# A binary convolution and gated state-space block over sixteen images: one reload buffer given to x, channel sums next to the gating, and sign bands shifted by one row, one unit ahead

## Chip, cores and metric

The kernel runs on one core of one Trainium2 chip. The metric is the device time of one execution in microseconds (us).

## What is computed

x is 16 x 112 x 112 x 256 in fp32. There are two layers, both with a residual:

```python
# _gn: normalize over H, W and 8 channels (32 groups)
x = x + _L0_conv_ref(_gn(x), L0_conv_kernel)   # depthwise 3x3 of sign(x) with sign(kernel)
x = x + _L1_conv_ref(_gn(x), ...)
# _L1_conv_ref(x): m, max over channels after a channel gate (sigmoid of two small
# matmuls on spatial mean and max); a scan over the 12544 pixels of an image with 16
# states gives y; a 7x7 convolution of channel mean and max gives s;
# x2 = xc * sigmoid(y) + xc * sigmoid(s); batch norm over all images; gamma, beta; relu
```

Only the sign of the group-normalized x enters the first convolution, that is, x compared with its group's mean.

## The kernel before, in words

Channels lie on the 128 partitions, in two halves (`j` = 0, 1). Pixels lie along the free dimension. The program has three blocks: the first reads x, makes x1 = x + convolution, writes it to `x1_scratch` in DRAM and computes the channel features; the second runs the scan of the second group of images and the batch statistics; the third computes and writes the output. The change is in the first block.

An image is cut into two parts, upper and lower half (`part`), and each part into seven units of eight rows (`u`, `RT` = 8, `TP` = 896 pixels). A convolution handles both parts at once: a sign element holds sign(upper) + 1024 * sign(lower) in fp16, so one matmul serves both parts. `image(i)` exists for each engine as a loop over `h` = 0 to 13 with `u, j = divmod(h, 2)`. What the engines do at pass h of image i, in the order of the code:

- PE: the convolution of (u, j), 18 matmuls (L1338), into `turn[h % 2]`; in the middle of it (from h = 2 on) the transposes of tile 2(h-2) of image i+1 (`turn_tile`, L1244); then the channel sums of strip h-5 (`channel_sums`, L1277); the transposes for the maximum over channels of the same strip (`blocks_back`, L1291); then tile 2(h-2)+1 of the next image. After h = 13 the last four tiles, `blocks_back` and `channel_sums` of strip 9, and the group means (L1250).
- ACT: evacuates the tile (L750), packs the convolution (L758), copies the channel sums (`average`, L813), evacuates the second tile, squares x1 of the unit before (L766), gates strip h-3 (`apply_gate`, L795 and L799).
- DVE: signs (`make_signs`, L961 and L976) of unit u+2, the maximum of the two channel halves of strip h-4 (`max_halves`, L1117), reductions over channels of strip h-5 (`reduce_blocks`, L1128), adds the convolution to x and takes the maximum (L1022, L1028), and gates one channel half of strip h-3 (`gate_half`, L1107) when the strip's number is 2 to 9. For the other strips ACT gates both halves. At h = 9 come three reductions of sign counts over edges (L985 to L990), then small steps that end in the sum of the convolution.
- SP: issues all DMAs, in order: the x load for a later pass (`load_next_x`, L569), the store of unit h-1 (L589), the load of strip h-1 (`load_g`, L584), and the channel sums of two strips to DRAM (L594).

A "strip" is 896 pixels of the image before (all 256 channels), read back from `x1_scratch` for gating, since the gate needs the statistics of the whole image. `strip_at(i, h, lag)` gives the strip h - lag of image i-1, and for h < lag one of image i-2. Strips live in a ring of four buffers `xg` in `xc`; x lives in a ring of three buffers in `stage`, which starts again with each image. A load into the strip ring waits until maximum and sum of the strip four back are made; an x load waits until the tiles of three loads back are turned. The channel sums of strip c go to `turn[c % 2]`, so at pass h to the half that the convolution of this pass doesn't use, once that has been packed.

After h = 13 DVE runs `image_sums`, `reduce_blocks` of strip 9, `sums_of_x` (L942) and `mean_of_x` (L951) of the next image, then signs of (0, 0) and (1, 0), `image_squares`, signs (0, 1), `image_variance`, signs (1, 1) and `attention_inputs`, which makes `fc_in`. Between variance and attention inputs ACT computes a logarithm and an exponential. PE's `hidden` matmul (L1260) in h = 1 waits for `fc_in`; the tile of h = 2 waits for `gate_argument` (DVE, L1083), which runs in h = 1 behind the signs of that pass.

In the first image, all 14 x loads and 28 tiles come ahead of the loop, and SP then issues the small parameter loads (`scol`, L612: 40 of them) and the bands before it enters `image(0)`. In the last image there is no next x; PE and DVE do parts of the second stage for the first group of images instead (a spatial convolution, `delta_step`).

## Time and profile before

| | us |
|---|---|
| median of 3 runs | 3481.12 |
| lowest and highest | 3471.48, 3544.35 |
| the profiled execution's own time | 3476.38 |
| its span, first to last instruction | 3474.7 |
| mean granted TensorE clock (share of full) | 0.832 |

The profile is of one execution. PE is the matmul engine, DVE the vector engine, ACT the scalar engine, POOL GpSimd and SP the engine that issues DMAs. In a timeline each line has the start in us from the span's beginning, the duration (overlaps with the next are possible), engine, line of the kernel, operation, output and inputs with their shape, and in brackets the idle time before it and what ended it.

### The profile page before, as it was taken

Reading aid. Unit: us, or ns where it says so; the run is one execution under the profiler, and the core shown is the slowest. Engines: PE = TensorE matmul, PEld = TensorE weight load, DVE = VectorE, ACT = ScalarE, POOL = GpSimd, SP = SyncE. Lnnn points to the kernel's source line nnn. Section 1 sums busy time; section 2 is a strip of 40 time slices with the busy share of each in tenths; the row PEclk is TensorE's granted clock in tenths of the full one; section 3 lists DMA queues with packets and bytes.
Section 4 is the critical chain, followed back from the end, with each engine's and each line's share of the span. In section 5 each row is a group of like instructions: output and inputs, shape, how many; then the busy total and the mean of one; then the engine's idle time right before and its main releaser. Section 6 shows DMA issues by size and latency. Waiting matters only on the chain. (4 is left out here: it accounts for less than half of the span.)

```text
span 3474.7 us, 50996 instructions
## 1 busy us (share of the span) xinstructions
PE 2596.4 (75%) x17105; PEld 1661.0 (48%) x17105; DVE 3053.3 (88%) x4395; ACT 2693.6 (78%) x3748; POOL 19.9 (1%) x23
## 2 busy tenths in 40 slices
PE   4899999999999998999877333333377767777676
PEld 3565555655556555566443010000255555555555
DVE  5689989999999998999886599999898899899997
ACT  3788887878888888888674287777788888888887
POOL 1000000000000000000000000000000000000000
PEclk8999999999999999999998555555577787777777
DMA  5898888988889888898765399999499999999998
GB/s 177 316 406 346 352 340 355 396 343 351 350 353 404 350 347 344 350 405 346 254 205 133 87 414 416 416 416 414 198 423 427 427 418 418 419 419 421 420 421 340
DMA packets 258888, 1227.99 MB, mean 353 GB/s; under 512 B 36421, under 2 KB 45537, under 8 KB 244353
## 3 DMA queue, kind: packets, MB, share of 16 engines
q1 hardware_dynamic: 258688, 1225.40, 89.0%
q8 instruction: 117, 1.92, 0.2%
q14 instruction: 83, 0.67, 0.1%
HBM read 805.14 MB, written 420.17 MB: 353 GB/s over the span
## 5 line engine op out<-in xcount | busy, mean ns | idle before, releaser
L1338 PE MATMUL psum<-signs,taps 128*128 128x448 f16 x4032 | 876.6, 362 | 49.1 <-DVE signs L976 44.9
L1759 PE MATMUL psum<-ident,xt 128*128 128x128 f32 x3136 | 560.5, 348 | 281.0 <-ACT stage L1793 232.5
L1759 PEld LDWEIGHTS psum<-ident,xt 128*128 128x128 f32 x3136 | 498.7, 212 | 367.2 <-ACT stage L1793 309.2
L1439 PE MATMUL psum<-signs,picked 12*128 12x448 bf16 x896 | 328.8, 510 | 356.1 <-DMA signs<-gate_scratch 287.3
L1338 PEld LDWEIGHTS psum<-signs,taps 128*128 128x128 f16 x4032 | 395.3, 100 | 381.0 <-issue 48.1
L1793 ACT ACTIVATE stage<-psum 128x512 f32<-128x512 f32 x784 | 407.1, 612 | 173.7 <-DMA out_dram<-stage 149.4
L1814 DVE SCALAR_TENSOR_TENSOR xc<-xt,curs,psum 128x1792 f32<-128x1792 f32 x224 | 456.1, 2077 | 85.7 <-PE psum L1439 81.2
L750 ACT ACTIVATE xt<-psum 128x896 f32<-128x896 f32 x416 | 377.9, 912 | 162.9 <-PE psum L1244 162.7
L1623 DVE SCALAR_TENSOR_TENSOR xc<-xt,curs,psum 128x1792 f32<-128x1792 f32 x224 | 455.6, 2078 | 49.5 <-PE psum L1439 34.4
L1244 PE MATMUL psum<-ident,stage 128*128 128x128 f32 x3136 | 416.5, 277 | 76.6 <-DMA stage<-x_dram 43.7
L1561 ACT ACTIVATE xc<-xc 128x1792 f32<-128x1792 f32 x224 | 380.1, 1697 | 113.6 <-DVE xc L1623 113.6
L1829 DVE TENSOR_TENSOR xt<-xc,xt 128x1792 f32<-128x1792 f32 x224 | 442.6, 2018 | 0.0
L1028 DVE CUSTOM_DVE_ANT_0 xt<-scratch,xt 128x896 f32<-128x896 int8 (+1 forms) x416 | 436.1, 1085 | 0.0
L1244 PEld LDWEIGHTS psum<-ident,stage 128*128 128x128 f32 x3136 | 364.9, 143 | 118.7 <-DMA stage<-x_dram 50.2
L1781 ACT ACTIVATE xc<-xc,bn,curs 128x1792 f32<-128x1792 f32 x224 | 411.3, 1900 | 8.6 <-DVE xc L1814 8.4
L766 ACT ACTIVATE hsum<-xt,nmean 128x1792 bf16<-128x1792 f32 x208 | 370.4, 1781 | 0.7
L1439 PEld LDWEIGHTS psum<-signs,picked 12*128 12x128 bf16 x896 | 86.7, 117 | 562.5 <-DVE xc L1623 380.1
L1128 DVE TENSOR_REDUCE pmax<-psum 128x4 f32<-128x512 f32 x448 | 257.7, 617 | 73.3 <-PE psum L1291 73.2
L758 ACT ACTIVATE scratch<-psum,border 128x896 int16<-128x896 f32 x224 | 223.9, 1000 | 82.8 <-PE psum L1338 82.4
L1117 DVE TENSOR_TENSOR stage<-xc 128x896 f32<-128x896 f32 x224 | 243.9, 1089 | 27.4 <-ACT xc L795 19.5
L976 DVE SCALAR_TENSOR_TENSOR signs<-xt,mean,signs 128x896 f16<-128x896 f32 x208 | 240.3, 1155 | 7.4
L1291 PE MATMUL psum<-ident,stage 128*128 128x128 f32 x1568 | 223.8, 282 | 24.1 <-ACT pmax_rows L806 13.8
(199 smaller groups left out, 2205.9 us busy)
## 6 DMA issues: line engine op xcount, KB each, us to landing
xt<-x_scratch SPq DMA_DIRECT2D x210, 1792.0 KB
stage<-x_dram SPq DMA_DIRECT2D x224, 896.0 KB, 9.0
out_dram<-stage SPq DMA_DIRECT2D x112, 1792.0 KB, 13.7
xc<-x_scratch SPq DMA_DIRECT2D x210, 896.0 KB, 8.3
x_scratch<-xt SPq DMA_DIRECT2D x208, 896.0 KB, 7.5
x_scratch<-last_unit SPq DMA_DIRECT2D x16, 896.0 KB, 6.9
signs<-ssm_scratch SPq DMA_DIRECT2D x28, 448.0 KB, 4.6
signs<-gate_scratch SPq DMA_DIRECT2D x217, 10.5 KB
```

The costliest lines, as they stand in the source:

```text
L750: nc.scalar.activation(dst, src, ACT.Identity, scale=PACK if part else 1.0, accum_out=xsum_p[:, j, 2 * u + part:2 * u + part + 1]).then_in ...
L1028: nc.vector.tensor_tensor_reduce(out=px, in0=conv, in1=px, scale=1.0 / PACK if part else 1.0, scalar=-3.0e38, op0=ALU.add, op1=ALU.max, ac ...
L1244: ins = nc.tensor.transpose(ring[:, t * P:(t + 1) * P], xin[b][:, t, j * P:(j + 1) * P], ident[:, :])
L1338: return nc.tensor.matmul(turn[h % 2][:, b * 512:b * 512 + HB], taps[:, j, t, :], signs[:, j, r:r + RT // 2, dw:dw + W], start=t == 0, sto ...
L1439: last = nc.tensor.matmul(dst[:, b, :], picked[:, b * P:(b + 1) * P], gate_rows[:, s * BW:(s + 1) * BW], start=True, stop=True)
L1561: nc.scalar.activation(u, u, ACT.Square, accum_out=g2_p[:, n, j, bass.ds(it, 1)]).then_inc(squared3, 1)
L1623: nc.vector.scalar_tensor_tensor(fours(xc[n % 2][:, j, :]), fours(slots[s][:, j, :]), curs[:, h, j:j + 1], gate_ps3[n % 2], ALU.add, ALU.mult,
L1759: last = nc.tensor.transpose(out_ps[k % 4][:, v * C + j * P:v * C + (j + 1) * P], block_in, ident[:, :])
L1781: nc.scalar.activation(u, u, ACT.Relu, bias=bn[:, 7, j:j + 1], scale=curs[:, h, NJ + j:NJ + j + 1]).then_inc(relu_made, 1)
L1793: nc.scalar.activation(outs[n % 2][:, 2 * k:2 * k + 2, :].rearrange("p t c -> p (t c)"), out_ps[k % 4], ACT.Identity).then_inc(staged, 1)
L1814: nc.vector.scalar_tensor_tensor(fours(xc[n % 2][:, j, :]), fours(slots[s][:, j, :]), curs[:, h, j:j + 1], gate_ps4, ALU.add, ALU.mult).th ...
L1829: nc.vector.tensor_tensor(x1, u, x1, ALU.add).then_inc(x2_made, 1)
```

## The change

It has three parts. (1) `xin` gets a fourth buffer, the second half of `xc[1]`, and the strip ring shrinks from four buffers to three. The x ring now runs on across images, each x load is issued one pass earlier relative to its use, and the first x load of the next image goes out in pass 13; for image 1 it goes out ahead of the small parameter loads. (2) `channel_sums` and `average` of a strip come one pass earlier (lag 4 for 5); `sum_ps` takes the other half of `turn` by strip number, which at a given pass is the same as before. The sum of strip 9 thereby moves from the image's end into pass 13. (3) A sign band is shifted down by one row, so that band u ends with the row below unit u: band 0 has nine rows, bands 1 to 4 have eight, band 5 has seven and band 6 seven; the first row of unit 6 gets two instructions of its own with a count of their own (`NS + 8`), since it may lie in another buffer. Band u is all that the convolution of unit u needs beside the earlier ones, so bands are made one unit ahead: passes 1 to 11 make one each, three are made at the image's start in place of four. The edge reductions go from pass 9 to 11, the count steps from passes 10 to 13 to passes 12 and 13.

```diff
+        NX = 4
...
         xg = [xc[b // 2][...][:, b % 2 * SP:(b % 2 + 1) * SP].rearrange(
-            "p (j n) -> p j n", j=NJ) for b in range(4)]
+            "p (j n) -> p j n", j=NJ) for b in range(3)]
+        xin.append(xc[1][:, :, :].rearrange("p j n -> p (j n)")[:, SP:2 * SP].rearrange("p (t c) -> p t c", c=C))
...
         def sum_ps(c):
-            return turn[c % 2][:, 0:SQ]
+            return turn[(c + 1) % 2][:, 0:SQ]
...
         def sign_at(u, j):
-            return 2 * j + u if u < 2 else NJ * u + j
+            return NJ * u + j
...
                 def load_next_x(i, k):
-                    sp.wait_ge(turned, i * NTILE + 2 * (k - 3) + 2)
+                    sp.wait_ge(turned, i * NTILE + 2 * (k - NX) + 2)
                     load_x(i, k)
...
-                    if i * NP + c >= 4:
-                        sp.wait_ge(maxed, i * NP + c - 3)
-                        sp.wait_ge(summed, i * NP + c - 3)
+                    if i * NP + c >= 3:
+                        sp.wait_ge(maxed, i * NP + c - 2)
+                        sp.wait_ge(summed, i * NP + c - 2)
...
-                for p in range(3, NP):
+                for p in range(NX, NP):
                     load_next_x(0, p)
+                load_next_x(1, 0)
 
                 for src, col in ((A_d[0, :], 0), (B_w_d[:, 0], 1), (B_b_d, 2), (C_w_d[:, 0], 3), (C_b_d, 4)):
...
                     if more:
-                        sp.wait_ge(turned, i * NTILE + NTILE)
-                        for p in range(3):
-                            load_x(i + 1, p)
+                        for p in range(1, NX):
+                            load_next_x(i + 1, p)
                     for h in range(NP):
-                        if h >= 3 and more:
-                            load_next_x(i + 1, h)
+                        if h >= NX - 1 and more and (i + 2 < NB or h < NP - 1):
+                            load_next_x(i + 1 + (h + 1) // NP, (h + 1) % NP)
...
             # ACT
-                        if (at := strip_at(i, h, 5)) and h >= 1:
+                        if at := strip_at(i, h, 4):
                             average(*at)
...
                     square(i, NU - 1, 1, first)
-                    if more and channels:
-                        average(i - 1, 9)
                     inverse_deviation(i)
...
             # DVE
-                    for u in range(NS):
+                    for u in (*range(NS), NS + 8):
                         nc.vector.tensor_reduce(coef[:, :, part, u], kval[:, :, :], AX, ALU.add).then_inc(coef_steps, 1)
...
+                def band_rows(u):
+                    return u * RT + (u > 0), (u + 1) * RT + (u < NU - 2)
...
+                    if u == NU - 2:
+                        row = signs[:, j, 1 + (NU - 1) * RT:2 + (NU - 1) * RT, 1:1 + W]
+                        compare(row, x_rows(i, j, NU - 1, 1, 0, 1), mean64[:, j:j + 1], ALU.mult, PACK).then_inc(row_steps, 1)
+                    r0, r1 = band_rows(u)
+                    rows = signs[:, j, 1 + r0:1 + r1, 1:1 + W]
+                    compare(rows, x_band(i, j, u, 1), mean64[:, j:j + 1], ALU.mult, PACK).then_inc(sign_steps, 1)
+                    if u == NU - 2:
+                        dve.wait_ge(row_steps, i * NJ + j + 1)
+                        nc.vector.scalar_tensor_tensor(
+                            row, x_rows(i, j, NU - 1, 0, 0, 1), mean, row, ALU.is_ge, ALU.add,
+                            accum_out=counts[:, j, NS + 8:NS + 9])
                     dve.wait_ge(sign_steps, base + 1)
                     nc.vector.scalar_tensor_tensor(
-                        rows, x_rows(i, j, u, 0, 0, RT),
+                        rows, x_band(i, j, u, 0),
                         mean, rows, ALU.is_ge, ALU.add, accum_out=counts[:, j, u:u + 1]).then_inc(signs_made, 1)
...
-                        if u + 2 < NU:
-                            make_signs(i, u + 2, j)
+                        if h >= 1 and u + 1 < NU:
+                            make_signs(i, u + 1, j)
...
-                        if h == 9:
+                        if h == 11:
                             edge_counts(i)
...
                         make_signs(i + 1, 0, 0)
-                        make_signs(i + 1, 1, 0)
+                        make_signs(i + 1, 0, 1)
                     image_squares(i)
                     if more:
-                        make_signs(i + 1, 0, 1)
+                        make_signs(i + 1, 1, 0)
                     image_variance(i)
-                    if more:
-                        make_signs(i + 1, 1, 1)
                     attention_inputs(i)
...
             # PE
-                        pe.wait_ge(signs_made, i * NP + sign_at(u if u == 0 else min(u + 1, NU - 1), j) + 1)
+                        pe.wait_ge(signs_made, i * NP + sign_at(u, j) + 1)
                         if not (first and h < 2):
                             pe.wait_ge(unpack_in, i * NP + h - 1)
-                        if strip_at(i, h, 6):
-                            pe.wait_ge(averaged, (i - 1) * NP + h - 5)
+                        if strip_at(i, h, 5):
+                            pe.wait_ge(averaged, (i - 1) * NP + h - 4)
...
-                            pe.wait_ge(signs_made, i * NP + sign_at(1, j) + 1)
                             for t in range(9):
...
-                        if (at := strip_at(i, h, 5)) and h >= 1:
+                        if at := strip_at(i, h, 4):
                             pe.wait_ge(unpack_in, i * NP + h)
                             channel_sums(*at)
+                        if (at := strip_at(i, h, 5)) and h >= 1:
                             blocks_back(*at)
...
                         if channels:
                             blocks_back(i - 1, 9)
-                            pe.wait_ge(evacuated, (i + 2) * NTILE)
-                            channel_sums(i - 1, 9)
                         group_sums(i + 1)
```

## Rows read from the trace of the kernel before

**Rows 1.** The page: busy us (share of the span) x instructions.
```profile
PE 2596.4 (75%) x17105; PEld 1661.0 (48%) x17105; DVE 3053.3 (88%) x4395; ACT 2693.6 (78%) x3748; POOL 19.9 (1%) x23
```

**Rows 2.** Busy time of each engine in one stretch, granted clock, DMA share, GB/s.
```profile
950.00:1060.00 110.00, 101.65 (x813) 64.95 (x811) 101.42 (x208) 91.98 (x143) 0.00 (x0) 0.98 0.92 362
```

**Rows 3.** Timeline of DVE: start, us, line, idle before. An image's first sum.
```profile
258.40 0.17 DVE L942 TENSOR_REDUCE xsum<-xsum_p 128x4 f32<-128x28 f32 x1
...
1014.54 0.18 DVE L942 TENSOR_REDUCE xsum<-xsum_p 128x4 f32<-128x28 f32 x1
...
1662.09 0.17 DVE L942 TENSOR_REDUCE xsum<-xsum_p 128x4 f32<-128x28 f32 x1
```

**Rows 4.** Timeline of DVE, units 5 to 9 of that image.
```profile
1065.21 0.74 DVE L1107 TENSOR_SCALAR xc<-xc,cur,gbias 128x896 f32<-128x896 f32 x1
1072.06 0.74 DVE L1107 TENSOR_SCALAR xc<-xc,cur,gbias 128x896 f32<-128x896 f32 x1
...
1092.60 0.62 DVE L985 TENSOR_REDUCE counts<-signs 128x4 f32<-128x448 f16 x1
1093.68 0.75 DVE L1107 TENSOR_SCALAR xc<-xc,cur,gbias 128x896 f32<-128x896 f32 x1
```

**Rows 5.** Timeline of PE, units 5, 6 and 12.
```profile
1060.38 0.55 PE L1291 MATMUL psum<-ident,stage 128*128 128x128 f32 x3 [1.06 <-ACT pmax_rows L806]
1065.82 0.96 PE L1277 MATMUL psum<-xc,over_c 128*32 128x224 f32 x16
...
1106.47 0.96 PE L1277 MATMUL psum<-xc,over_c 128*32 128x224 f32 x16
```

**Rows 6.** Timeline of PE and ACT, unit 4.
```profile
1050.78 0.96 PE L1277 MATMUL psum<-xc,over_c 128*32 128x224 f32 x16
...
1053.54 0.92 ACT L750 ACTIVATE xt<-psum 128x896 f32<-128x896 f32 x1 [0.32 <-PE psum L1244]
...
1057.25 1.12 ACT L799 ACTIVATE xc<-xc,gbias,cur 128x896 f32<-128x896 f32 x1
1058.28 0.90 ACT L750 ACTIVATE xt<-psum 128x896 f32<-128x896 f32 x1
```

**Rows 7.** Timeline of PE, ACT and DVE, from one image into the next.
```profile
1011.18 1.75 PE L1244 MATMUL psum<-ident,stage 128*128 128x128 f32 x14 [0.98 <-DMA stage<-x_dram]
1014.08 1.13 ACT L795 ACTIVATE xc<-xc,gbias,cur 128x896 f32<-128x896 f32 x1
1015.88 1.07 DVE L961 TENSOR_SCALAR signs<-xt,mean 128x112 f16<-128x112 f32 x3
1027.04 0.25 PE L1260 MATMUL psum<-fc_in,w 128*16 128x2 f32 x4 [0.95 <-DVEq L1076]
1027.08 0.69 DVE L961 TENSOR_SCALAR signs<-xt,mean 128x896 f16<-128x896 f32 x1
1028.89 1.08 DVE L1117 TENSOR_TENSOR stage<-xc 128x896 f32<-128x896 f32 x1
1034.28 0.98 PE L1244 MATMUL psum<-ident,stage 128*128 128x128 f32 x7 [0.73 <-DVEq L1084]
```

**Rows 8.** Waits of PE between 110 and 1800 us: in total, times, longest.
```profile
PE psum L1244 <- DMA stage<-x_dram: 18.8, 12, 2.4
```

**Rows 9.** Timelines of SP's queue and of PE, images 0 and 1.
```profile
48.92 7.03 SPq L612 DMA_DIRECT2D scol<-A_dram  x8
78.84 3.02 SPq L569 DMA_DIRECT2D stage<-x_dram  x3
87.23 1.75 PE L1244 MATMUL psum<-ident,stage 128*128 128x128 f32 x7 [11.72 <-DMA stage<-x_dram]
93.11 2.09 PE L1338 MATMUL psum<-signs,taps 128*128 128x448 f16 x10
98.08 2.07 PE L1338 MATMUL psum<-signs,taps 128*128 128x448 f16 x10
```

**Rows 10.** The page, DMA issues: count, KB each, median us to landing.
```profile
xc<-x_scratch SPq DMA_DIRECT2D x210, 896.0 KB, 8.3
```

More of the change, by code:

```diff
@@ L235, in binary_conv_then_gated_ssm_block @@
         taps_made = sem("taps_made")
-        x_in = [sem(f"x_in{b}") for b in range(3)]
+        x_in = [sem(f"x_in{b}") for b in range(NX)]
         turned = sem("turned")
@@ L266, in binary_conv_then_gated_ssm_block @@
         gate_in = sem("gate_in")
-        g_in = [sem(f"g_in{b}") for b in range(4)]
+        g_in = [sem(f"g_in{b}") for b in range(3)]
         gated = sem("gated")
@@ L603, in _ @@
                     sp.dma_start(dst[:], src).then_inc(params_in, 16)
-                for p in range(3):
+                for p in range(NX):
                     load_x(0, p)
                 sp.dma_start(lsa[:, :], lsa_d.broadcast_to([H, KS * KS * 2])).then_inc(lsa_in, 16)
-                for p in range(3, NP):
+                for p in range(NX, NP):
                     load_next_x(0, p)
+                load_next_x(1, 0)
                 for src, col in ((A_d[0, :], 0), (B_w_d[:, 0], 1), (B_b_d, 2), (C_w_d[:, 0], 3), (C_b_d, 4)):
@@ L862, in _ @@
                 apply_gate(NB - 2, 11)
-                average(NB - 2, 9)
                 gate_exp(NB - 1)
@@ L907, in _ @@
                 for part in range(2):
-                    for u in range(NS):
+                    for u in (*range(NS), NS + 8):
                         nc.vector.tensor_reduce(coef[:, :, part, u], kval[:, :, :], AX, ALU.add).then_inc(coef_steps, 1)
-                    steps.n += NS
+                    steps.n += NS + 1
                     row = NS + part
@@ L961, in compare, with x_band @@
                     return nc.vector.tensor_scalar(dst, x, mean, v, ALU.is_ge, op1)
+                def x_band(i, j, u, part):
+                    if u == NU - 1:
+                        return x_rows(i, j, u, part, 1, RT)
+                    r0, r1 = band_rows(u)
+                    at = part * H2 * W
+                    return xt[:, j, at + r0 * W:at + r1 * W].rearrange("p (h w) -> p h w", w=W)
+                def band_rows(u):
+                    return u * RT + (u > 0), (u + 1) * RT + (u < NU - 2)
                 def make_signs(i, u, j):
@@ L1133, in _ @@
                 mean_of_x(0)
-                for h in range(4):
-                    make_signs(0, h % 2, h // 2)
+                for h in range(NJ + 1):
+                    make_signs(0, *divmod(h, NJ))
                 def image(i):
@@ L1393, in _ @@
                 hidden(NB - 1)
-                channels_late(NB - 2, 9)
+                blocks_back(NB - 2, 9)
                 gate(NB - 1)
```

37 lines of the change are left out of this document (17 added, 20 removed).

## Prediction

> **What bounds the kernel now.** I read the page's busy times first: DVE is busy for 88% of the span, more than any other engine [rows 1]. Such shares mix stages, so next I took windows of equal length over the first part of the program. In each the granted clock is 0.97 or 0.98 and both PE and DVE are above 90%, as in the one shown: 101.65 and 101.42 of 110 us [rows 2]. The change touches only this part, which ends near 1780 us. Then I timed one image by the DVE instruction that starts an image's group means: from 258.40 to 1662.09 us are 13 images, 107.98 us each, and one of them starts at 1014.54 [rows 3]. The timelines of PE, DVE and ACT inside that image say what sets its length. I call one pass of the loop over h (one channel half of a unit) a unit here.
>
> From unit 6 on DVE repeats its work every 6.85 us with no idle time (its gate_half at 1065.21 and at 1072.06) [rows 4]. PE starts its channel sums at 1065.82 in unit 6 and at 1106.47 in unit 12, 6.78 us a unit [rows 5]. Both are full; DVE falls 0.07 us a unit behind PE, which costs nothing since it makes no signs in units 10 to 13 and catches up there. In units 2 to 5 ACT gates both channel halves and is full too; it waits 0.32 us in the unit shown [rows 6]. Between images there is a chain: transposes (0.98 us late for an x load), evacuations, means, signs, PE's convolution, and later PE's waits for fc_in and for gate_argument [rows 7].
>
> **The change part by part.** All is compared with the profiled execution: span 3474.7 us, time 3476.4 us, which is 4.7 us below the median of the runs, 3481.1.
>
> *1. x loads one unit ahead, within an image.* PE waited for x 12 times between 110 and 1800 us, 18.8 us in all and 2.4 at most [rows 8]. These lie at ends of images, where the last tiles follow each other with no convolution between, as at 1011.18 [rows 7]. The load now goes out a unit (6.8 us) sooner, more than the longest wait, so I take the waits as gone. What is late next is ACT: it evacuates the last tiles one after another until 1014.08, which ends at best 0.1 us sooner, while the means began at 1014.54 [rows 3, 7]. So of a wait of 0.98 only some 0.49 comes back, and I take off 0.49 from each: 18.8 - 12 x 0.49 = 12.9 us gained. Bounds: 0 (the load comes no sooner) and 18.8.
>
> *2. The first image's small loads.* After image 0's last x load SP issues 40 loads of one column each and a few more, from 48.92 us on, and image 1's first three x loads only at 78.84; PE stood still 11.72 us for them until 87.23 [rows 9]. Now image 1's first x load goes out ahead of the small ones. PE can do the unit that uses it, and then waits for the second one, still behind them. One unit there is 98.08 - 93.11 = 4.97 us [rows 9]: 5 us gained. The start itself has four loads in flight instead of three, and SP comes to the small loads when 22 tiles are turned, with one load less ahead of it at some 2.3 us (0.92 MB at 400 GB/s). I take 3 us, between 0 and 5. Together 8 us (5 to 10).
>
> *3. Signs one unit ahead, at the image's start.* DVE makes three bands there instead of four. The two nine-row bands take some 0.17 us more each. One band of 1.8 us (1027.08 to 1028.89 is one [rows 7]) goes from in front of fc_in, but it was also the work that covered ACT's logarithm and exponential, now open with 0.5 us. So fc_in comes 1.8 - 0.5 - 0.2 = 1.1 us sooner than 1027.04. Unit 1 ends that much sooner on PE; then a wait of 0.40 us for the maximum goes, and the one of 0.73 us at 1034.28 for gate_argument, since no band stands ahead of it. Unit 2 is about 2.1 us ahead.
>
> *4. Channel sums right after gating.* PE now waits in unit h for gating that ACT and DVE finish at the end of their unit h-1. Queued behind that wait on PE are blocks_back and the turn of tile n+1, for which ACT's next evacuation waits: a closed loop. Its length from rows 6: channel sums to evacuation 1053.54 - 1050.78 = 2.76 us, from there to the end of both gatings 1058.28 - 1053.54 = 4.74 us. That is 7.5 us with both halves, and 1.03 less, 6.5, with one. The latter stays under PE's 6.78. The former exceeds ACT's own work in such a unit (4.74 and some 2.2 for the other evacuation, pack and average: 6.9) by up to 0.6 in units 3 and 4, and PE first meets the wait 0.8 us late; in unit 5 it waited 1.06 us for the maximum's rows anyway [rows 5]. Of the 2.1 us ahead 1.5 are given back: unit 6 starts 0.6 us ahead, at 1065.2.
>
> *5. DVE becomes part of the loop.* From unit 6 to 13 channel sums also wait for DVE's gate_half of the unit before; so far DVE could be late there for free. It now has bands in units 10 and 11, the three edge reductions (1093.68 - 1092.60 = 1.08 us [rows 4]) in unit 11 instead of 9, and two extra row instructions for each channel half in units 8 and 9. A row compare adds 0.19 us (1015.88: two of them and a band's compare of 0.69 in 1.07 [rows 7]); the row's sum with its accumulator I take at 0.25. The bands of these units and the last two are a row shorter, 0.2 us less. From the end of unit 5 to that of unit 11: 2 x 6.85 + 2 x (6.85 + 0.44 - 0.2) + 2 x 6.65 + 1.08 = 42.3 us. Unit 5 ends on DVE near 1063.9: its last reduction follows the blocks that PE makes after the wait of unit 5, now 0.6 us sooner than 1060.38 and done at 1060.3, and 3.6 us of DVE's own work come after. So unit 12's sums start at 1063.9 + 42.3 + 0.1 = 1106.3, against 1106.47 before [rows 5]: all but 0.2 us is given back. With bands and reductions shared out over two channel halves and 14 full images I count 0, with bounds of -1.2 us an image (DVE not binding, the head start kept) and +1.2 us (0.1 to 0.2 us of latency a unit in the loop): -17 and +17 us.
>
> The Trainium skill speaks against my price for the rows. Its page "VectorE: DVE Perf Modes", section "The TRN2 errata — SBUF-src ops pay a fixed extra latency per instruction", has a fixed part of about 150 cycles at 0.96 GHz. For 112 elements that makes 0.27 us, an estimate, and four an image 1.1 instead of 0.9: 3 us more over the kernel. The 0.19 us at 1015.88 disagrees, for compares issued back to back.
>
> *6. A ring of three for the gated strips.* A strip's load now waits for the maximum of the strip three back, made 1.5 us later in the unit than the sum it used to wait for, and SP stands still with store and x load queued behind it. Some one and a half units remain until the gating, over a landing time of 8.3 us [rows 10]. At an image's start one such load moves by some 12 us, to about 1027; its strip is gated after 1040. I count nothing; without that cover each image would lose some 2 us.
>
> *7. The rest.* Moved count steps lie on DVE's idle time in units 12 and 13, the added reductions for coef under image 0's loads. After the last image the strip load that waited for sum 9 waits for maximum 10, 1.5 us later, against one channel sum less on PE: nothing. In the last image DVE also computes the deltas and binds more: 1.5 us lost, bounds 0 and 4. All after 1830 us is unchanged.
>
> Sum: 3476.4 - 12.9 - 8 + 0 + 1.5 = 3457.0.
>
> **Rivals.**
> *A, the loop of parts 4 and 5 costs more (slower than before).* Its place is PE's wait ahead of channel sums in the units that gate one half there. For it: DVE's gate_half of 1065.21 ends after PE's channel sums of 1065.82 have begun, and DVE's unit is longer than PE's [rows 4, 5]. Against: ACT's loop of 6.5 leaves 0.2 us. With 0.25 us more in ten units it is 2.5 us an image, 35 us over 14: 3457 + 35 = 3492. From 1.4 us an image on the change is no gain.
> *B, DVE doesn't bind.* If PE and ACT set units 6 to 13 and DVE follows, the head start survives, 1.2 us an image: 3457 - 17 = 3440. Against: DVE shows no idle time in units 6 to 9.
> *C, the extra x buffer brings no earlier x.* Three transfers of 0.92 MB in a unit of 6.78 us are 406 GB/s. If the DMA engines can't give more, the waits stay and only the 5 us of part 2 remain: 3471. Against: their share is 0.92, not 1, with a mean of 362 GB/s over a window that holds an image's end, where little is moved [rows 2]. On this the page "DMA: Bandwidth & Descriptors", section "Where 436 GB/s comes from", of the Trainium skill says that transfers between HBM and SBUF are held to about 358 GB/s. By that rule C would hold; the trace's 362 as a mean disagrees.
>
> **How the numbers follow.** Forecast 0.5, A 0.15, B 0.17, C 0.18. The forecast's own range is 3445 to 3470; B reaches down to 3440, C up to 3471, A to 3492. For 8 in 10 I take 3434 to 3488. A measurement of this kernel tells about 2% from no change, 70 us. Only B with three times its price would reach that: 0.04. Slower by 70 us needs over 6 us an image in A: 0.04. Within 2%: 0.92.
>
> **What would show it.** Right: PE's waits for x at image ends are gone and images lie near 107.1 us apart; the stop at 87 us is near 6 us long and one unit later; PE waits ahead of channel sums, for ACT in units 3 and 4 and for DVE from unit 9 on, up to 1 us in unit 12; DVE has no idle time from unit 6 to 11. Wrong: images of 109 us with those waits longer (A), images under 106.3 (B), x waits as before (C), or a lower granted clock in the first part.

## The result and the profile after

The change makes the kernel slower. The median went from 3476.3 us (4 runs, with those above) to 3609.02 us (3608.52 to 3660.04); the ratio is 1.042, with a 95% interval of 1.036 to 1.049. By the medians alone it is 1.038. The forecast was 3457 us, with a range from 3434 to 3488: both the sign and the size were wrong. Some executions of one and the same kernel take 1 to 2% longer at a lower mean granted clock, such as the one of 3660 us here (0.812 against 0.819); the medians take them in, and the ratios leave out those that are over 1.5% above the fastest. The profiled execution took 3608.6 us, with a span of 3606.9.

Where the time is can be read from three instants. These are the DVE instructions that start an image's group means, the same as in [rows 3], in the timeline of DVE of the changed kernel:

```profile
242.08 0.18 DVE L943 TENSOR_REDUCE xsum<-xsum_p 128x4 f32<-128x28 f32 x1
...
1071.95 0.18 DVE L943 TENSOR_REDUCE xsum<-xsum_p 128x4 f32<-128x28 f32 x1
...
1778.61 0.18 DVE L943 TENSOR_REDUCE xsum<-xsum_p 128x4 f32<-128x28 f32 x1
```

The first stands 16.3 us earlier than its partner of 258.40: what lies before image 2 became shorter. From the first to the last are the same 13 images, 118.19 us each, where it was 107.98: 132.8 us lost. From the last to the end of the span are 1828.3 us, where it was 1812.6: 15.7 lost in the last image and what follows it. The three make 132.2 us, the difference of the two spans.

The page's busy lines of PE and DVE and the window that answers to [rows 2] show engines that have become idle, not busier. DVE's 3053.3 us have grown by 50, but its share has fallen from 88 to 86%:

```profile
PE 2622.9 (73%) x17105; PEld 1679.9 (47%) x17105; DVE 3102.9 (86%) x4493; ACT 2695.7 (75%) x3748; POOL 19.7 (1%) x23
```

```profile
950.00:1060.00 110.00, 94.88 (x736) 60.75 (x735) 96.84 (x198) 82.82 (x130) 0.00 (x0) 0.94 0.88 327
```

PE and DVE are each some 5 to 7 us shorter of work in 110 us, and the DMA's share and the granted clock are lower. So a wait has come in. The view of waits from 110 to 1800 us (total, times, longest) names it:

```profile
PE psum L1354 <- ACT hsum L817: 96.4, 28, 8.1
ACT hsum L817 <- DMA feat_scratch<-hsum: 91.8, 13, 8.6
DVE stage L1137 <- ACT xc L803: 90.5, 14, 8.4
```

Three engines wait some 7 us each, once an image (the first row's 28 times hold short ones too): one event, passed on. The reader should look for the one that waits for no engine. That is ACT's `average` (L817), which waits for a DMA, the store of strip sums. The timeline around one of them, of SP, ACT, PE and DVE:

```profile
1112.06 1.07 SPq L598 DMA_DIRECT2D feat_scratch<-hsum  x1
...
1118.88 0.36 ACT L817 ACTIVATE hsum<-psum 128x224 f32<-128x224 f32 x1 [7.15 <-DMA feat_scratch<-hsum]
...
1119.38 3.89 PE L1354 MATMUL psum<-signs,taps 128*128 128x448 f16 x10 [6.65 <-ACT hsum L817]
...
1123.98 1.09 DVE L1137 TENSOR_TENSOR stage<-xc 128x896 f32<-128x896 f32 x1 [7.03 <-ACT xc L803]
```

SP issues the store at 1112.06, and ACT is released at 1118.88, 6.8 us later: the store's landing time. After it PE's convolution of ten matmuls takes 3.89 us, where it takes 2.08 elsewhere. The mean granted clock from 1119 to 1123 us is 0.50, which is the lower level, 1.2 GHz; from 1100 to 1112, ahead of the pause, it was 1.00.

This is the cause in the code. There are two strip-sum buffers, `srow[s % 2]`, and an image has seven pairs of strips. So its last pair (s = 6) and the next image's first (s = 0) use the same buffer. `sums_out` of pair 6 goes out in pass 4 (even passes, lag 6). `average` of strip 0, which needs the buffer back, came in pass 5 before and comes in pass 4 now. The pass between the two had been the cover of the store's landing.

The second loss stands in DVE's groups with the shapes kept apart (busy, mean ns of one, idle before). L962 is the compare of a band, and 1008, 896 and 784 elements are nine, eight and seven rows of 112:

```profile
L962 DVE TENSOR_SCALAR signs<-xt,mean 128x896 f16<-128x896 f32 x128 | 87.8, 686 | 4.5 <-DVE gbias L1117 0.6
...
L962 DVE TENSOR_SCALAR signs<-xt,mean 128x784 f16<-128x784 f32 x48 | 49.3, 1028 | 0.0
...
L962 DVE TENSOR_SCALAR signs<-xt,mean 128x1008 f16<-128x1008 f32 x32 | 40.3, 1259 | 0.0
...
L962 DVE TENSOR_SCALAR signs<-xt,mean 128x112 f16<-128x112 f32 x64 | 16.3, 277 | 0.3
```

Seven rows take longer than eight. From 784 to 1008 elements the compare grows by 0.231 us, 1.03 ns an element.

### The profile page after: what moved, and what is told of

It reads as the page before. It is cut to its first block and busy times, and to the rows that moved or that the text cites. A ratio compares the mean times of both kernels' runs of the same rounds, so it can differ in the third digit from the quotient of the medians.

```text
span 3606.9 us, 51095 instructions
## 1 busy us (share of the span) xinstructions
PE 2622.9 (73%) x17105; PEld 1679.9 (47%) x17105; DVE 3102.9 (86%) x4493; ACT 2695.7 (75%) x3748; POOL 19.7 (1%) x23
## 5 line engine op out<-in xcount | busy, mean ns | idle before, releaser
L1354 PE MATMUL psum<-signs,taps 128*128 128x448 f16 x4032 | 905.7, 371 | 164.1 <-ACT hsum L817 109.9
L1354 PEld LDWEIGHTS psum<-signs,taps 128*128 128x128 f16 x4032 | 404.2, 102 | 512.2 <-issue 186.9
L1260 PE MATMUL psum<-ident,stage 128*128 128x128 f32 x2352 | 311.1, 276 | 26.0 <-POOL counts L723 17.5
L1260 PEld LDWEIGHTS psum<-ident,stage 128*128 128x128 f32 x2352 | 275.0, 143 | 53.4 <-POOL counts L723 17.5
L1293 PE MATMUL psum<-xc,over_c 128*32 128x224 f32 x3584 | 217.7, 360 | 57.9 <-DVE xc L1127 31.1
L996 DVE SCALAR_TENSOR_TENSOR signs<-xt,mean,signs 128x896 f16<-128x896 f32 (+2 forms) x208 | 238.3, 1146 | 6.3
```

Source lines behind the costliest of these rows:

```text
L1260: ins = nc.tensor.transpose(ring[:, t * P:(t + 1) * P], xin[b][:, t, j * P:(j + 1) * P], ident[:, :])
L1354: return nc.tensor.matmul(turn[h % 2][:, b * 512:b * 512 + HB], taps[:, j, t, :], signs[:, j, r:r + RT // 2, dw:dw + W], start=t == 0, sto ...
```

## The experiments

Images apart means the mean of the same 13 images, from the group means of each version's profiled execution. "To image 2" and "the end" are the stretches before and after them, in us.

| version | median | ratio to before, 95% | to image 2 | images apart | the end |
|---|---|---|---|---|---|
| before | 3471 to 3476 | 1 | 258.4 | 107.98 | 1812.6 |
| after | 3609.0 | 1.042 (1.036 to 1.049) | 242.1 | 118.19 | 1828.3 |
| a_store | 3505.6 | 1.009 (1.008 to 1.011) | 242.0 | 110.65 | 1824.1 |
| a_parity | 3505.7 | 1.010 (1.009 to 1.012) | 241.6 | 110.65 | 1822.9 |
| a_split | 3584.6 | 1.032 (1.030 to 1.034) | 240.7 | 116.79 | 1828.2 |
| a_both | 3486.6 | 1.006 (1.003 to 1.010) | 240.9 | 109.29 | 1823.1 |
| b_sums | 3589.0 | 1.034 (1.032 to 1.035) | 254.6 | 116.09 | 1822.4 |
| b_sums_store | 3485.7 | 1.003 (1.000 to 1.006) | 253.4 | 109.01 | 1815.0 |
| a_old_signs | 3486.1 | 1.003 (0.999 to 1.006) | 242.2 | 109.34 | 1823.9 |
| b_signs | 3468.9 | 0.997 (0.994 to 1.000) | 251.2 | 107.75 | 1818.8 |
| b_signs_split | 3444.4 | 0.992 (0.990 to 0.994) | | | |
| b_prologue | 3457.8 | 0.995 (0.991 to 0.998) | 243.2 | 107.58 | 1817.6 |
| b_win | 3433.0 | 0.988 (0.986 to 0.990) | 237.1 | 106.02 | 1816.4 |
| a_swap | 3482.6 | 1.004 (1.001 to 1.007) | 238.6 | 109.04 | 1827.7 |
| a_swap_small | 3475.7 | 1.003 (1.000 to 1.007) | 231.3 | 109.07 | 1823.2 |
| a_old_swap_small | 3495.0 | 1.006 (1.005 to 1.008) | 233.9 | 110.12 | 1825.5 |

Names with a_ start from the changed kernel, those with b_ from the kernel before. Each ratio is against executions of the kernel before that were taken with that version. Of b_signs_split only the times are used, since its trace is of an execution of 3507.77 us.

The stretches before and after the 13 images vary from one execution to the next. Up to image 0's means b_sums and b_sums_store run the same instructions as the kernel before. They reach them at 56.18 and 57.06 us, the trace of the kernel before at 60.11. And b_prologue changes nothing at the end of the program, but its end is 5.0 us longer than before. So a difference of 4 or 5 us between two versions in these two columns is no finding.

**The store of the strip sums.** Three versions. First, on the changed kernel, the store goes out one pass sooner:

```diff
-                        if h % 2 == 0 and (at := strip_at(i, h, 6)):
+                        if h % 2 == 1 and (at := strip_at(i, h, 5)):
                             sums_out(at[0], at[1] // 2)
...
-                for s in range(4, NS):
+                for s in range(5, NS):
                     sums_out(NB - 2, s)
```

> The changed kernel with one edit: SP issues the store of two strips' sums one pass sooner (odd passes, lag 5, instead of even passes, lag 6). Theory W (the wait of ACT's average for the strip-sum buffer, 106 us at L817 in the changed kernel's trace over 14 images, is what made images 118 us long): the 7.2 us waits at pass 4 of each image go, and with them most of the slowdown, about 7 us for each of 13 or 14 images: 3609 - 95 = 3514 us (3500 to 3525). Rival G (the closed loop of gating and channel sums costs it in every unit, and the wait for the store only takes up time that would be lost elsewhere): above 3570 us. Rival R (the compares over an odd number of rows are the main cost): above 3570 us too, with DVE's band compares unchanged at 1.03 and 1.26 us.

It took 3505.56 us, 103 less than the changed kernel, and images are 7.54 us shorter. Theory W holds, G and R fall as main causes. Second, the same wait brought into the kernel before, by the near sums alone:

```diff
-            return turn[c % 2][:, 0:SQ]
+            return turn[(c + 1) % 2][:, 0:SQ]
...
-                        if (at := strip_at(i, h, 5)) and h >= 1:
+                        if at := strip_at(i, h, 4):
                             average(*at)
```

> The kernel before with one part of the change alone: channel sums and average one unit nearer to the gating (lag 4), with the turn buffer's other half; three x buffers, four strip buffers and signs two units ahead as before. Theory W: the store's wait of about 7 us an image appears here alone, and the images grow by most of it: 3476 + 80 to 100 = 3565 us (3545 to 3580). Rivals R and X (the odd bands, or the smaller ring of gated strips, make the loss): within 15 us of 3476 us.

It took 3589 us, more than expected, and the wait is there. From its view of waits and its ACT timeline:

```profile
ACT hsum L813 <- DMA feat_scratch<-hsum: 83.3, 13, 7.1
```

```profile
1114.10 0.36 ACT L813 ACTIVATE hsum<-psum 128x224 f32<-128x224 f32 x1 [6.75 <-DMA feat_scratch<-hsum]
```

So this one part of three costs 116 us by itself, where the whole change costs 133. Third, with the store left late, the two buffers taken in turn over all images, so that the next image's first pair gets the other one:

```diff
-                                 srow[s % 2][0:P:32, :, :]).then_inc(sum_out[s % 2], 16)
+                                 srow[(i * NS + s) % 2][0:P:32, :, :]).then_inc(sum_out[(i * NS + s) % 2], 16)
...
-                    s, b = c // 2, c // 2 % 2
+                    s, b = c // 2, (i * NS + c // 2) % 2
...
-                        act.wait_ge(sum_out[b], i * (16 * turns(b, 2, NS)) + 16 * (s // 2) + 1)
+                        act.wait_ge(sum_out[b], 16 * ((i * NS + s) // 2) + 1)
```

> The changed kernel with its store left where it is, and the two strip-sum buffers taken in turn over all images instead of anew in each (an image fills 7, so as it is its last and the next one's first use the same buffer). Theory W in its narrow form (ACT waits in pass 4 only because the buffer it needs is the one whose store has just gone out; the other one is long free): the 7 us waits go without any store being made sooner, images 110.6 us apart, time 3505 us (3495 to 3515), as with the early store. Rival V (the early store helped in another way, by what it moved in SP's queue, and the late store itself is what hurts): above 3570 us.

It took 3505.72 us, with images of 110.65 us, the same as with the early store. Rival V falls: a late store does no harm where nothing needs its buffer.

**The odd bands.** On the changed kernel, and together with the early store:

```diff
-                    compare(rows, x_band(i, j, u, 1), mean64[:, j:j + 1], ALU.mult, PACK).then_inc(sign_steps, 1)
+                    band = x_band(i, j, u, 1)
+                    for a, b in (((0, 1), (1, r1 - r0)) if (r1 - r0) % 2 else ((0, r1 - r0),)):
+                        compare(rows[:, a:b, :], band[:, a:b, :], mean64[:, j:j + 1], ALU.mult, PACK).then_inc(sign_steps, 1)
+                        sign_count[0] += 1
```

> The changed kernel with one edit: a compare over a band of 9 or 7 rows is made as two, one row and then 8 or 6 rows; the waits stay otherwise. If the row count's parity sets the compare's rate, the 8 rows take 0.69 us and the 6 rows some 0.5 us, each with a row of 0.19 to 0.28 us ahead: a saving of some 0.3 us on each of four nine-row bands and 0.3 us on each of two seven-row bands an image. Theory W: the long wait for the strip-sum buffer stays, DVE is not what binds an image there, and the two nine-row compares at an image's start bring 0.3 to 0.7 us an image: 3609 - 5 to 10 = 3600 us (3590 to 3609). Rival R (DVE's slower compares are the main cost): below 3560 us.

> Both edits together: the store of the sums one pass sooner, and odd bands compared as one row and an even rest. Theory W with the bands as the second, small part: 3505 us by the store alone less 1 to 2 us an image for the bands, which bind once the long wait is gone: 3480 to 3500 us. If all other terms of my prediction were right (the waits for x gone, the prologue 8 us or more shorter, the rest nothing), it must come near 3457 us. Rival G (the loop costs as well): above 3500 us.

a_split took 3584.59 us, 24 less than the changed kernel; a_both took 3486.64, 19 less than a_store. Images are 1.4 us shorter in both. I had expected 5 to 10 us for the first, so the bands' work counts even where the long wait stays. (The expectation also has the counts exchanged: an image has two compares over nine rows and four over seven.) The groups of DVE in a_split:

```profile
L962 DVE TENSOR_SCALAR signs<-xt,mean 128x896 f16<-128x896 f32 x160 | 109.9, 687 | 4.9 <-DVE gbias L1122 1.0
...
L962 DVE TENSOR_SCALAR signs<-xt,mean 128x672 f16<-128x672 f32 x48 | 27.6, 574 | 0.0
```

Eight rows and six rows take 0.687 and 0.574 us: 0.5 ns an element, half of what the odd counts pay. a_both is at 3487 and not at 3457, so other terms were wrong too.

**The near sums without the store's wait.** The kernel before with the edit of b_sums and that of a_store:

> The kernel before with the channel sums one unit nearer to the gating and the store of the sums one pass sooner; x ring, strip ring and signs as before. It isolates what the near sums cost once the store's wait is gone. Theory L (the closed loop of gating and sums in units 2 to 5 costs 1.7 us an image, and the sums of strip 10, moved from the image's end into unit 0, stand ahead of fc_in in PE's queue): images 109 to 111 us apart against 108.0, total 3472 + 15 to 40 = 3500 us (3487 to 3512). Rival N (near sums cost nothing once the store is early, and what is left over in the version with both repairs comes from the x ring or the signs): 3472 us, within 8.

It took 3485.7 us, at the edge of theory L: 12 us more than before in place of 15 to 40, with images 1.03 us longer in place of 1 to 3. Rival N falls. One more reading of this trace was not expected. Its x ring still has three buffers, and its view of waits holds no row of PE's matmuls waiting for x any more, whose waits were 18.8 us in [rows 8].

**The x ring.** The changed kernel with the early store and the old signs. It differs from b_sums_store in the x ring of four and the strip ring of three alone:

> The changed kernel without its signs' part (bands of 8 rows two units ahead, edge counts in unit 9 as before), with the early store of the sums: x ring of four, strip ring of three, near sums. If DVE's share of the changed loop (bands and edge counts in units 10 and 11: PE waited 0.9 us for DVE in unit 12 of the version with both repairs) goes with the signs, images are 1.0 us shorter than that version's 109.3: 3487 - 13 = 3474 us (3465 to 3480). If signs one unit ahead pay for themselves at the image's start by more than that, it is above 3487 us.

It took 3486.07 us. Against b_sums_store the table has 11.2 us less up to image 2, 0.33 us more in each of 13 images (4.3 us), and 9 us more at the end. So beside the near sums the fourth x buffer pays only in the prologue, and the rest of the same pair of edits takes all of it back. That the shorter strip ring does this is read from the traces; no run has the two rings apart, or the x ring of four without the near sums.

Within images the shorter ring holds up SP. A strip's load now waits for the maximum of the strip three back, and the store of sums stands right behind it in SP's queue. In b_sums_store that store goes out 32.2 us after an image's means (mean of the 13 images), in a_both 33.8, in a_old_signs 35.6. In the last ACT has to wait for it again, in every image (waits from 240 to 1662 us):

```profile
ACT hsum L816 <- DMA feat_scratch<-hsum: 14.2, 13, 2.6
```

In that stretch b_sums_store and a_both have no such wait. What the ring takes at the end is seen in the timeline of ACT in a_both, where the gating of strip 12 is late for its load (a_old_signs has the same wait, 3.15 us; b_sums_store has none):

```profile
1798.56 1.13 ACT L799 ACTIVATE xc<-xc,gbias,cur 128x896 f32<-128x896 f32 x1 [3.22 <-DMA xc<-x_scratch]
```

Then the clock falls. The windows from 1800 to 1820 us, of a_both and of the kernel before, with the granted clock ahead of the last two columns:

```profile
1800.00:1820.00 20.00, 16.50 (x114) 7.73 (x114) 15.73 (x16) 14.79 (x22) 0.00 (x0) 0.68 0.27 64
```

```profile
1800.00:1820.00 20.00, 16.29 (x168) 8.61 (x168) 19.55 (x20) 17.13 (x25) 0.00 (x0) 1.00 0.51 128
```

PE is busy as long in both, but for 114 matmuls in place of 168: it stands partly at 1.2 GHz. The strip ring is not the only way to get there: b_signs, with four strip buffers, has a granted clock of 0.50 from 1795 to 1800 us, where the kernel before has 1.00, and an end that is 6 us longer.

As to the expectation of the signs in a_old_signs: its 3486 us meet neither alternative, and its images are 109.34 us, those of a_both 109.29. Signs one unit ahead with even bands bring nothing in sum here, although they spare ACT the wait for the store.

**The signs' part alone,** on the kernel before, and the same with the split of a_split:

> The kernel before with the signs' part alone: bands of 9, 8, 8, 8, 8, 8, 7 rows one unit ahead, the row of the last unit made in units 8 and 9, the edge counts in unit 11. The odd bands' compares must take 1.03 and 1.26 us here too. Theory S (without near sums DVE is not in PE's loop from unit 6 on, so only the image's start pays, 0.6 us for the first nine-row band, against 1 us from fc_in made sooner): 3472 us, within 15, images within 1 us of 108.0. Rival D (the 2.5 us of DVE work an image count in full wherever they lie): 3472 + 35 = 3507 us.

> The kernel before with the signs' part alone, odd bands compared as one row and an even rest. The split was worth 24 us on the changed kernel and 19 us on the one with the early store; the signs' part with slow odd bands was worth 4 us on the kernel before. If the odd bands' slow compares hid a gain of the signs' part: 3469 - 20 = 3449 us (3440 to 3457), images 106.0 us apart. If the fastest version's gain comes from the small loads and the split only pays beside them: 3465 us or more.

b_signs took 3468.93 us (theory S), b_signs_split 3444.41: 27 us less than its runs of before, 3471.3. The odd bands had hidden a real gain.

**The small loads.** My own edit of the kernel before: the 42 small parameter loads, three in each pass of image 0, in place of all in a row:

```diff
+                        if i == 0:
+                            for dst, src in smalls[3 * h:3 * h + 3]:
+                                sp.dma_start(dst, src).then_inc(p2_params, 16)
```

> The kernel before with one edit of mine: the 42 small parameter loads, which stand in SP's queue between image 0's last x load and image 1's first three, are issued three at a time in image 0's passes. PE stood 11.7 us there for image 1's first x load. Theory P (that queue is what makes most of the changed kernel's prologue shorter): PE's wait at 87 us falls to some 2 us and the time to 3472 - 8 to 10 = 3463 us. Rival Q (the x loads themselves limit there, behind image 0's): the wait stays and the time is 3472 us, within 3.

It took 3457.79 us, 15 less, where 8 to 10 were expected. PE's wait at 87 us [rows 9] is gone altogether: from image 0's means to those of image 1 are 81.7 us, where it was 94.4. Image 0's means come at 57.05 us, 3 us sooner than at 60.11, but that is no second gain of the spread loads: b_sums and b_sums_store, with all small loads in a row as before, have them at 56.18 and 57.06. The trace of the kernel before has a late start.

**The order of PE's steps.** In a_both, `blocks_back` ahead of the channel sums:

```diff
-                        if at := strip_at(i, h, 4):
-                            pe.wait_ge(unpack_in, i * NP + h)
-                            channel_sums(*at)
                         if (at := strip_at(i, h, 5)) and h >= 1:
                             blocks_back(*at)
+                        if at := strip_at(i, h, 4):
+                            pe.wait_ge(unpack_in, i * NP + h)
+                            channel_sums(*at)
```

> The version with both repairs (early store, odd bands split; images 109.3 us apart, 3487 us) with PE's two steps of a unit exchanged: blocks_back before the channel sums. Theory L (what is left of the loss is a closed loop: behind PE's wait for the gating stand blocks_back and the turn of tile n+1, for which ACT's evacuation and then the next gating wait; a unit with both halves on ACT took 7.7 to 8.0 us against 7.0 to 7.3 before): with 0.98 us of blocks_back ahead of the wait the loop is 6.8 us long, PE's waits ahead of the sums (36 us for ACT, 14 us for DVE) fall to under a third, and images are 1.5 to 2.5 us shorter: 3487 - 20 to 33 = 3460 us (3450 to 3470). Rival F (the sums of strip 10 ahead of fc_in, and the x ring's three places for strips, make the rest): within 6 us of 3487.

It took 3482.58 us, 4 less, which is within the spread of the two versions' runs and within rival F's bounds; 3450 to 3470 was expected. But the trace shows more. PE's waits for the gating ahead of the sums are gone: of 35.5 us for ACT and 13.9 us for DVE in a_both, 0.9 us is left. In unit 5 another wait has grown. PE's timeline in one image, where a_both waits 0.3 us:

```profile
1047.98 0.55 PE L1312 MATMUL psum<-ident,stage 128*128 128x128 f32 x3 [1.89 <-ACT pmax_rows L810]
```

The loop is open, and in unit 5 PE stands behind the same full ACT, at the maximum's rows. PE's weight loads wait 27.9 us for these rows in images 2 to 14, where it was 7.1. That is 1.6 us an image, of more than 3 that the exchange freed.

What this wait sets off costs more than the wait. In five of the 13 images the clock stays up behind it, and these take 107.6 to 108.2 us, 1.4 less than a_both's 109.3: near the 1.5 to 2.5 of theory L. In the other eight the clock falls to its lower level right behind the wait, and they take 109.3 to 110.2 us. The windows, some 47 to 51 us after the means, of an image of the first kind and the next one, of the second kind (the clock ahead of the last two columns):

```profile
1049.00:1053.00 4.00, 4.00 (x37) 2.68 (x26) 3.96 (x9) 2.90 (x4) 0.00 (x0) 1.00 1.01 365
1157.00:1161.00 4.00, 4.00 (x28) 2.47 (x21) 4.00 (x8) 1.35 (x4) 0.00 (x0) 0.57 1.00 349
```

In a_both, which has no such wait, the clock stays at 1.00 there in all 13. So the loop was sized about right, and what a_swap's images still lose against the 107.98 us of the kernel before is lost in those with the lower clock. Why it falls behind waits of 1.8 to 2.0 us in eight images and stays up behind waits of 1.7 to 2.0 in five, the traces don't show.

> The version before this one with the 42 small loads issued three at a time in image 0's passes. There PE still stood 4.9 us for image 1's second x load; that goes, and the small loads no longer lie beside image 0's last x loads. If the two gains add: 5 us less than the exchange alone, some 3455 us (3445 to 3465). If the x ring of four has already taken what the small loads cost: within 2 us of it.

3475.72 us, 7 less than a_swap, near the expected 5, from an end of the prologue that comes 7.2 us sooner; the total of 3455 is missed with a_swap's. The clock falls in unit 5 in nine of its 13 images.

> The changed kernel with the old signs, the early store, the exchanged steps and the spread small loads. It tells what the signs' part is worth beside the x ring, once the loop is open: with the old signs DVE has nothing to do for signs in units 10 to 13 but makes four bands at the image's start. The pair with the loop closed came out equal (3486 and 3487 us). Expected the same here: within 5 us of the version with the new signs, some 3455 us; if the new signs' head start at the image's start was only hidden by the loop, this one is 10 us or more slower.

It took 3495.01 us, a miss of 40 us. In its trace ACT waits for the store of sums again, 19.5 us in 13 times, and PE's convolution 30.6 us for `average`. The exchange alone does not make that wait: a_old_signs has it too, 14.2 us in 13 times, and a_swap_small, exchanged and with the new signs, has 0.9 us. The mark of both is the old signs over a strip ring of three. In both the store goes out 35.6 us after the means, where it is 33.8 in a_both and 33.4 in a_swap_small, because it stands in SP's queue behind a strip's load that waits for DVE's maximum. So the early store has lost 2 us of its cover. A version with old signs, the exchange and a strip ring of four would test this; none was run.

**A version that beats both.** From what held: the kernel before, with the signs one unit ahead, odd bands split, and the small loads spread. Rings, sums and store stay as they were:

> The kernel before with the small loads spread over image 0's passes, and the signs' part with odd bands compared as one row and an even rest; rings, sums and store as before. From its parts: the spread loads gave 15 us (3473 to 3458), the signs' part 4 us with slow odd bands, within its noise. If they add and the split brings the nine-row bands' 0.3 us each at the image's start: 3458 - 4 - 4 = 3450 us (3440 to 3460). If the signs' part is worth nothing: 3458 us.

It took 3433.0 us, ratio 0.988 (0.986 to 0.990): 41 us less than before and 176 less than the changed kernel. Expected were 3440 to 3460, by too small a value for the split; the 15 us of the small loads and the 27 of the signs with even bands simply add. Images are 106.02 us apart, by these instants of its DVE timeline:

```profile
237.12 0.17 DVE L946 TENSOR_REDUCE xsum<-xsum_p 128x4 f32<-128x28 f32 x1
...
1615.39 0.17 DVE L946 TENSOR_REDUCE xsum<-xsum_p 128x4 f32<-128x28 f32 x1
```

PE still waits for x in it, and it is faster all the same:

```profile
PE psum L1268 <- DMA stage<-x_dram: 21.7, 14, 3.2
```

## Why the prediction was wrong

*Part 4, channel sums right after gating: the failed step.* The part followed the moved sums to what they wait for (the gating) and to what waits for them (the closed loop), but not to the second wait of `average`, `sum_out`, which stands right below its first in the function. The step was moved up to the pass in which its buffer's store goes out, and the sum of the forecast has nothing for that. Measured: 7.54 us an image by a_store, 98 us over 13. Rival A named the right side, but with another mechanism, 0.25 us in ten units. The closed loop itself was sized about right: I had 7.5 us for a unit with two halves, and in a_both PE's sums of units 2 to 5 are 7.73, 8.01 and 7.74 us apart (they start 22.23, 29.96, 37.97 and 45.71 us after the image's means). From unit 2 to 6 a_both takes 1.7 us more than before (1.5 forecast).

*Part 3, the bands.* I priced a nine-row band, both of its instructions, at 0.17 us more than one of eight. Its compare alone took 0.57 more (1.259 against 0.686) and its second instruction 0.12. A seven-row compare took 0.34 more instead of less, and with its second instruction the band took 0.22 more: part 5's "0.2 us less" with the wrong sign. With two nine-row and four seven-row bands an image this is 2 x 0.38 + 4 x 0.27 = 1.8 us above the split forms (0.19 us for the row by my price), of which 1.4 us showed. The Trainium skill has the rule that I did not weigh. Its page "VectorE: DVE Perf Modes", section "What auto-detection actually checks", lets an operation with a single source, source and destination both in SBUF, run at twice the rate if their outermost dimensions, leaving out those of one, are both even or equal. This case agrees if the nine or seven rows of the source, which lie without a gap in x, count as one run, while the destination keeps its row count: 0.5 ns an element for eight and six rows, 1.03 for nine and seven. No run tests that reading by another layout of the source.

*Part 3, the head start.* It exists: b_win and b_signs_split have it (27 us in the latter). Beside the near sums it is nothing. In a_both PE starts unit 2's sums 22.23 us after the means, against 22.18 in the kernel before; I had said 2.1 us ahead. The waits of [rows 7] went as described, but a channel sum had come into unit 0 (0.96 us), with 0.57 us of wait for its average behind it, ahead of fc_in in PE's queue. That is strip 10's sum, which came from unit 1; part 7 counted strip 9's sum leaving the image's end, and nothing counted strip 10's arrival.

*Part 5, DVE in the loop.* In a_both PE waits 0.90 us for DVE in unit 12, and from unit 6 to 12 it takes 41.60 us against 40.65: 0.95 lost against the forecast's 0.4. Kind right, size low. Of the two prices for a row, the instruction's own duration is 0.277 us (the mean in the groups above), near the 0.27 that the prediction worked out from the Trainium skill's page "VectorE: DVE Perf Modes", but in a_both four compares, three rows and one band of eight, take 1.25 us together at 1007.52 us: a row adds (1.25 - 0.69) / 3 = 0.19, as I took it.

*Part 1, the x waits.* They are gone, but b_sums_store shows them gone with three buffers as well. So beside the near sums my 12.9 us belong to no ring. Rival C's result, that the fourth buffer brings nothing within images, came true, but by another way than the DMA's rate, and so not by its reason. In the versions without near sums these waits remain (27.5 us in b_signs, 21.7 in b_win); what a fourth buffer would bring there was not run.

*Part 2, the prologue.* 16.3 us up to image 2 by the two traces, twice my 8; by a_old_signs against b_sums_store, which has no late start in it, 11.2. The start came 7.5 us sooner than in the trace of the kernel before, but 4 us sooner than in b_sums and b_sums_store, where I had 3. The stop of 11.72 us at 87 us became one of 4.88 at 78.96, 6.8 where I had 5. The rest, 2 us in image 1, I had not seen.

*Part 6, the ring of three.* "I count nothing" held within images to 0.33 us, though what the part described, SP standing still with the store behind it, came: it is the wait of 14.2 us in a_old_signs. At the program's end, where part 7 also said nothing, it is 9 us (a_old_signs against b_sums_store), of which up to 5 can be the spread between executions. In a_both 3.2 us are the wait for strip 12's load, and part of the rest is PE at its lower clock.

Put together for the changed kernel against the one before: 98 us store wait and 18 us odd bands in 13 images, 17 us that are left in them (13 x 1.31, a_both against before), 16 us at the end, 16 us won up to image 2. That makes 133, against 132.2 of the spans; the stretches add up by construction, so this shows where the time went and is no test of the causes. The 17 us divide by the table into 13 for the near sums with an early store (b_sums_store against before), 4 for the two rings (a_old_signs against b_sums_store) and nothing for the signs with even bands (a_both against a_old_signs).

## What to carry to other kernels

When a step is moved to an earlier pass, list every wait in it, and for each the pass in which its releaser is issued: a DMA that is issued in the same pass is a wait of its whole landing time, 6.8 us here. A ring of two that is indexed anew in each image with an odd count meets itself at the border, so index it through. Before the rows of a band change, look whether the count stays even in the operation that runs at the double rate, and when several parts come together, price each with the others' queues in place: here the signs' part is worth 27 us alone and nothing beside the near sums. Look at the granted clock image by image before a version is said to have gained nothing: a_swap's mean hides images that are 1.4 us shorter.

## What the runs showed that I had not expected

- A compare from f32 to f16 runs at 0.5 ns an element over 8 or 6 rows and at 1.03 ns over 9 or 7. The one with a second input (1155 ns for 896 elements) grows evenly, 1037 and 1272 for 784 and 1008.
- A store of a few sums takes 6.8 us from issue to release of ACT, about as long as the load of a strip of 896 KB (6.9 on the changed kernel's page).
- Spreading 42 small loads over 14 passes gave 15 us, more than PE's wait of 11.72 us for x behind them.
- After a pause of 6.65 us PE's next convolution ran at a granted clock of 0.50, 3.89 us for 2.08. In a_swap a wait of some 2 us was followed by such a fall in eight images of 13, and these images took 1.8 us longer than the other five.
